# The shared layer's first product and the router's of rounded parts, in a transformer kernel written for one core

## The chip, the core and the metric

The kernel runs on one core of a Trainium2 chip. The core has five engines that work side by side and wait for one another through semaphores: TensorE (PE in the profile; PEld is its weight load), VectorE (DVE), ScalarE (ACT), GpSimd (POOL) and SyncE (SP), whose queue here only issues DMAs. The metric is the time on the device of one execution, in microseconds.

## What is computed

A two-layer model over 16 tiles of 384 tokens, each token 256 numbers. Cut to what matters:

```python
h = edges_of_image_and_text_rows                      # 16 x 384 x 256
h = h + attention(layernorm(h))                       # 16 heads, local window of 128
h = h + top_k_block(layernorm(h))                     # rows of highest score through one product and gelu
h = h + state_space(layernorm(h))                     # a circulant recurrence over 256 states
xf = layernorm(h)
logits = xf @ router_w.T + router_b                   # 8 experts, the top two are taken
shared = gelu(xf @ shared_w1.T + b1) @ shared_w2.T + b2   # 256 -> 1024 -> 256
h = h + shared + sum_e(weight_e * ffn_e(xf))          # experts 256 -> 1024 -> 256
```

## The kernel before

Work goes tile by tile (NB = 16), T = 384 tokens in NT = 3 parts of P = 128. A tile is in one of three stages, and one pass of `sequence(b, ...)` on each engine interleaves them: the attention of tile b, the chain of tile b - 1 (block, state space, router, first shared product, "up"), the second shared product ("down") and the dispatch to experts of tile b - 2; also the head of tile b + 1 (edges, text, norm, queries, keys, values). `sequence` counts slots s = 0 to 32 (SLOTS = 33). In each slot `unit(b, s)` does a step of attention: scores on TensorE (L1624, L1625), their maximum on VectorE (L1150), exponentials on ScalarE (L819), turned probabilities (L1633) and products with the values (L1652). Everything else has its slot by constants such as TURN1 = 12, STATE = 14, CONV = 15, TURN2 = 27, UP = 28, LOGIT = 30. Each engine works through its own list strictly in order; nothing is reordered at run time. Tiles 2 to 13 run in a loop, 0, 1, 14 and 15 are written out; pass NB has the chain alone, with idle products (`keep_warm`, L1834) between the chain's steps. The passes with a chain and a head are those of b = 1 to 14.

What the change touches, in the order of a pass's end: in slot 27 TensorE turns the chain's normalised rows into the accumulator (L1689), ScalarE copies them to `xcT` (L839), VectorE's `keys(b + 1)` writes the rounded keys `k_hi` (L1118) and their rests `k_lo` (L1122), `query_rests` writes `q_lo` (L1129). SyncE's `stack` copies them head by head into `qs` and `ks` (L445, L451), in four groups (`PAIRS`), each with a semaphore `stacked[g]`; the attention units 2g and 2g + 1 are the first to read group g. In slot 28 TensorE does `logits(b - 1)` (L1773), in slot 30 `values(b + 1)` (L1600), whose third part writes to the keys' bank and waits for `k_lo`; then the turn of the context rows `cx` (L1667, after VectorE's L1163), `up(b - 1, 0)`, the output product (L1640), and `up(b - 1, f)` for f = 1 to 7 (L1703), after which the next pass begins. Each `up` writes one of two banks; ScalarE's `hidden_layer` (L855) reads it, and `up` f + 2 waits for that.

Products of fp32 operands show two records each. Operands of type F32R (rounded to fewer bits) show one. The experts' products already use rounded parts: with x = x_hi + x_lo, a product is w_hi x_hi + w_hi x_lo + w_lo x_hi (L1885 to L1889). `rot` and `cum` hold the state space's rotations and sums and, as `trial`, the unread outputs of the rank comparisons (L1221, L1224) with the constant tables `before` and `after`. In pass 0 VectorE also makes the eigenvalues and, in slots 2 to 10, their powers.

## Time and profile before

| | |
|---|---|
| median of three runs | 2078.8 us (2075.1 to 2082.78) |
| the profiled execution | 2077.58 us, span 2075.8 us |
| TensorE busy | 1955.6 us, 94% of the span |
| TensorE's weight loads | 1572.7 us, 76% |
| VectorE, ScalarE, GpSimd busy | 1337.9, 1071.3, 778.8 us |
| first shared product (L1703) | 512 records, 174.5 us busy |
| experts' stage | from about 1465 us to the end |

The columns of the rows below: in the order of time a row has the start (us from the span's start), the duration (of all instructions it merges, from the first start to the last end), the engine (SPq and ACTq are DMA issues), the line of the kernel, the operation, output<-inputs, shapes, the count, and in brackets how long the engine was idle before and what released it. Matmul records overlap; the distance of their starts is what they cost. A busy engine is not one at its peak, and idle time of an engine that sets no end costs nothing.

### The profile page before, as it was taken

The page shows a single profiled execution, that of the slowest core. Times are in us where ns is not written, and L with a number is a line of the kernel's source. Part 1 is how long each engine was busy: PE and PEld are TensorE (multiplying, and loading weights), DVE is VectorE, ACT ScalarE, POOL GpSimd, SP SyncE. Part 2 cuts the span into 40 slices and gives each one's busy share as a digit, 9 for nine tenths or more (in the row PEclk, how much of TensorE's full clock was granted, in tenths as well). Part 3 has the DMA queues.
Part 4 walks back from the last instruction along what each step waited for, and adds up shares of the span by engine and source line. Part 5 has one row for each costly group of instructions (what it writes and reads, how often), then busy time and mean ns, then how long its engine had stood idle before and what let it go on. Part 6 is the DMA issues. An engine that isn't in the chain of part 4 may idle for free.

```text
span 2075.8 us, 45068 instructions
## 1 busy us (share of the span) xinstructions
PE 1955.6 (94%) x13784; PEld 1572.7 (76%) x13864; DVE 1337.9 (64%) x3781; ACT 1071.3 (52%) x2509; POOL 778.8 (38%) x1269
## 2 busy tenths in 40 slices
PE   4779999999999999999999999888999999999997
PEld 3556667667676676666676766666999999999997
DVE  4667677676776776766767767655665555656553
ACT  0445556455455564555645545541554555555553
POOL 4013324333343233332432333304354455555544
PEclk8899999999999999999999999998999999999998
DMA  4221120211212202212022021110442232323222
GB/s 153 62 62 40 39 69 23 61 52 24 69 37 47 68 24 54 56 28 69 30 54 64 28 54 38 32 55 23 128 129 45 45 89 45 89 43 86 48 45 40
DMA packets 81091, 116.56 MB, mean 56 GB/s; under 512 B 20964, under 2 KB 61508, under 8 KB 78724
## 3 DMA queue, kind: packets, MB, share of 16 engines
q1 hardware_dynamic: 54372, 84.16, 14.6%
q0 software_dynamic: 23360, 27.91, 8.0%
q10 hardware_dynamic: 3312, 3.94, 0.7%
q8 instruction: 21, 0.34, 0.1%
q14 instruction: 26, 0.21, 0.0%
HBM read 51.58 MB, written 26.71 MB: 38 GB/s over the span
## 4 chain that ended last, share of the span: by engine, by line
PE 75%; issue 9%; DVE 8%; POOL 4%; ACT 1%; ACTq 1%; POOLq 0%; DVEq 0%; DMA 0%
PE ps L1888 14%; PE ps L1703 8%; PE ps L1716 7%; PE ps L1899 4%; PE ps L1900 4%; PE ps L1901 4%; PE ps L1633 4%; PE ps L1549 3%; PE ps L1625 3%; PE ps L1652 3%; PE ps L1577 2%; PE ps L1694 2%; PE ps L1754 2%; PE ps L1689 2%; PE ps L1624 2%
## 5 line engine op out<-in xcount | busy, mean ns | idle before, releaser
L819 ACT ACTIVATE prob<-ps,mx 128x256 f32<-128x256 f32 (+1 forms) x768 | 294.3, 440 | 188.7 <-DVE mx L1150 176.8
L1150 DVE TENSOR_REDUCE mx<-ps 128x2 f32<-128x512 f32 (+1 forms) x384 | 228.5, 596 | 206.7 <-PE ps L1625 196.8
L931 ACT ACTIVATE hid_hi<-ps,b 128x256 fp32r<-128x256 f32 x408 | 205.9, 505 | 276.3 <-PE ps L1888 276.3
L811 ACT ACTIVATE pT<-ps 128x512 f32<-128x512 f32 (+1 forms) x384 | 202.4, 532 | 136.2 <-PE ps L1633 123.5
L1479 DVE TENSOR_TENSOR hid_lo<-hid_full,hid_hi 128x256 fp32r<-128x256 f32 x408 | 170.9, 425 | 143.3 <-ACT hid_full L934 139.8
L732 POOL DMA_INDIRECT result<-yb,idx_o x102 | 176.8, 1734 | 164.1 <-DVE yb L1496 142.2
L1899 PE MATMUL ps<-w_hi,hid_hi 128*128 128x256 f32 x816 | 230.0, 282 | 0.0
L1900 PE MATMUL ps<-w_lo,hid_hi 128*128 128x256 f32 x816 | 225.5, 276 | 0.0
L1901 PE MATMUL ps<-w_hi,hid_lo 128*128 128x256 f32 x816 | 225.3, 276 | 0.0
L1633 PE MATMUL ps<-ident,prob 128*128 128x128 f32 x1280 | 207.3, 276 | 7.0 <-ACT prob L819 6.8
L934 ACT ACTIVATE hid_full<-ps,b 128x256 f32<-128x256 f32 x408 | 206.2, 505 | 0.0
L1625 PE MATMUL ps<-ks,qs 96*128 96x512 f32 (+1 forms) x384 | 199.0, 518 | 3.1 <-ACT prob L819 3.1
L676 POOL DMA_INDIRECT slot_rows<-pay,row_i x96 | 113.3, 1180 | 219.6 <-DVE tok L1339 195.1
L1633 PEld LDWEIGHTS ps<-ident,prob 128*128 128x128 f32 x1280 | 160.1, 143 | 44.6 <-ACT prob L819 13.7
L1716 PE MATMUL ps<-sw,hid 128*128 128x256 f32 x768 | 185.9, 387 | 2.3 <-ACT g L846 1.0
L1703 PE MATMUL ps<-xcT,sw 128*128 128x384 f32 x512 | 174.5, 495 | 0.0
L1888 PE MATMUL ps<-xg_hi,w_hi 128*128 128x256 f32 x816 | 165.1, 284 | 2.5 <-DVE xg_lo L1472 1.4
L1716 PEld LDWEIGHTS ps<-sw,hid 128*128 128x128 f32 x768 | 138.8, 190 | 34.2 <-issue 11.7
L1888 PE MATMUL ps<-xg_hi,w_lo 128*128 128x256 f32 x816 | 164.4, 283 | 0.0
L1888 PE MATMUL ps<-xg_lo,w_hi 128*128 128x256 f32 x816 | 164.4, 283 | 0.0
L1900 PEld LDWEIGHTS ps<-w_lo,hid_hi 128*128 128x128 f32 x816 | 153.4, 188 | 0.0
L1899 PEld LDWEIGHTS ps<-w_hi,hid_hi 128*128 128x128 f32 x816 | 153.3, 188 | 0.0
(283 smaller groups left out, 4114.5 us busy)
## 6 DMA issues: line engine op xcount, KB each, us to landing
w_raw<-in_w SPq DMA_DIRECT2D x16, 1024.0 KB
xin<-in_x SPq DMA_DIRECT2D x32, 384.0 KB
ks<-k_hi SPq DMA_DIRECT2D x256, 48.0 KB, 2.1
qs<-q_hi SPq DMA_DIRECT2D x120, 96.0 KB, 2.1
ks<-k_lo SPq DMA_DIRECT2D x128, 48.0 KB, 2.1
xn_rows<-xc SPq DMA_DIRECT2D x16, 384.0 KB, 2.5
result<-h SPq DMA_DIRECT2D x16, 384.0 KB
qs<-q_lo SPq DMA_DIRECT2D x60, 96.0 KB, 2.1
```

Source lines behind the costliest of these rows:

```text
L819: ins = act.activation(prob[:, s % PB, hh, w], ps[:, s % 2, hh * 2 * P + w.start:(hh + 1) * 2 * P], ACT.Exp, bias=mx[:, s % 2, hh:hh + 1])
L931: act.activation(hid_hi[:, f], ps[:, f % 4, 0:CHUNK], ACT.Gelu_apprx_tanh, bias=b1[half][:, f:f + 1])
L934: act.activation(hid_full[:, f % 4], ps[:, f % 4, 0:CHUNK], ACT.Gelu_apprx_tanh, bias=b1[half][:, f:f + 1]).then_inc(ehid_ready.sem, 1)
L1150: dve.tensor_reduce(mx[:, s % 2], sc, AX_X, ALU.max, negate=True).then_inc(max_done.sem, 1)
L1625: pe.matmul(dst, qs[:, r, m, i * P:(i + 1) * P], ks[:, r, :, m, keys], start=False, stop=True).then_inc(scores_done.sem, 1)
L1633: ins = pe.transpose(ps[:, 2 + u % 2, (2 * hh + k) * P:(2 * hh + k + 1) * P], prob[:, u % PB, hh, k * P:(k + 1) * P], ident[:])
L1703: ins = pe.matmul(ps[:, 6 + f % 2, 0:T], sw1[:, k, f * P:(f + 1) * P], xcT[:, k], start=(k == 0), stop=(k == KB - 1))
L1716: ins = pe.matmul(tile_out(i), hid[:, f, i * P:(i + 1) * P], sw2[:, f], start=(f == 0), stop=(f == FB - 1))
L1888: ins = pe.matmul(ps[:, f % 4, 0:CHUNK], w[half][:, k, cols], x[:, k], start=(n == 0), stop=(n == len(terms) - 1))
L1899: pe.matmul(out, hid_hi[:, f, rows], w2_hi[half][:, f], start=(f == 0), stop=False)
L1900: pe.matmul(out, hid_hi[:, f, rows], w2_lo[half][:, f], start=False, stop=False)
L1901: ins = pe.matmul(out, hid_lo[:, f, rows], w2_hi[half][:, f], start=False, stop=(f == FB - 1))
```

## The change

The router's and the first shared product take rounded parts. `sw1` is loaded into room of `hid` in pass 0, rounded on ScalarE in slot 12 and its rest taken on VectorE in slot 15; the router's weights are split before pass 1 into `rw_parts`, high and low parts side by side, so one product with `xcT_hi` gives both; a second one with `xcT_lo` adds to the high half, and VectorE adds the two halves and the bias. ScalarE's last copy of turned rows writes `xcT_hi`; VectorE's new `turned_rests` writes `xcT_lo`, between `k_hi` and `k_lo` (or by itself where there are no keys). On TensorE the first two parts of `values` go ahead of the logits, which move from slot 28 to 29. To make room, `k_hi` and `k_lo` share their memory with `rot`, `xcT_hi` with `xcT`, `xcT_lo` with `st`; the rank comparisons write to `st`, `xn` and `cum`; VectorE waits for all four `stacked` groups before it writes `rot` (slot 1 of pass 0, slot 14 of later ones); `before` and `after` become windows into one table each, `rank_cols` lies in `hb2`. The loads of the experts' biases move behind SyncE's pass NB.

```diff
 # memory
-        rank_cols = sb("rank_cols", [P, T])
-        before = sb("before", [P, NT, T], BF16)
-        after = sb("after", [P, NT, T], BF16)
+        before_w = sb("before_w", [P, T + 2 * P], BF16)
+        after_w = sb("after_w", [P, T + 2 * P], BF16)
+        before, after = ([w[:, (NT - 1 - i) * P:(NT - 1 - i) * P + T] for i in range(NT)] for w in (before_w, after_w))
+        rw_parts = sb("rw_parts", [P, KB, 2 * NE], F32R)
+        rw_hi, rw_lo = rw_parts[:, :, 0:NE], rw_parts[:, :, NE:2 * NE]
-        sw1 = sb("sw1", [P, KB, F])
+        sw1_hi = sb("sw1_hi", [P, KB, F], F32R)
+        sw1_lo = sb("sw1_lo", [P, KB, F], F32R)
-        k_hi = room("k_hi", [P, KB, T], F32R)
-        k_lo = room("k_lo", [P, KB, T], F32R)
+        with ExitStack() as shared:
+            xcT_hi = shared.enter_context(nc.sbuf_tensor("xcT_hi", [P, KB, T], F32R))
         xcT = room("xcT", [P, KB, T])
...
+        with ExitStack() as shared:
+            k_hi = shared.enter_context(nc.sbuf_tensor("k_hi", [P, KB, T], F32R))
+            k_lo = shared.enter_context(nc.sbuf_tensor("k_lo", [P, KB, T], F32R))
         rot = room("rot", [P, 4, T])
         cum = room("cum", [P, 2, T])
+        with ExitStack() as shared:
+            xcT_lo = shared.enter_context(nc.sbuf_tensor("xcT_lo", [P, KB, T], F32R))
         st = room("st", [P, 2, T])
...
+        rank_cols = hb2[:].rearrange("p i d -> p (i d)")[:, 0:T]
...
+        sw1 = place[:, 0:KB * F].rearrange("p (k n) -> p k n", k=KB)
 # SyncE: (sw1, t["sw1"]) leaves late_loads
             load_image(1)
+            sp.wait_ge(mats_read.sem, mats_read.at(0, 1))
+            sp.dma_start(sw1, t["sw1"]).then_inc(sw1_loaded.sem, 16)
             load_halo(1)
...
+            sequence(NB, True, True, False, False)
+            sp.wait_ge(hb2_ready.sem, hb2_ready.at(NB, 0))
             for half in range(2):
                 load_biases(half, half)
-            sequence(NB, True, True, False, False)
 # ScalarE
-                act.activation(xcT[:], ps[:, 6:8, 0:T], ACT.Copy).then_inc(xcT_ready.sem, 1)
+                act.activation((xcT if n < 2 else xcT_hi)[:], ps[:, 6:8, 0:T], ACT.Copy).then_inc(xcT_ready.sem, 1)
...
+            def round_shared():
+                act.wait_ge(sw1_loaded.sem, sw1_loaded.at(0, 16))
+                act.activation(sw1_hi[:], sw1, ACT.Copy).then_inc(sw1_rounded.sem, 1)
...
+                    if first and s == TURN1:
+                        round_shared()
 # VectorE
-                for i in range(NT):
-                    dve.tensor_scalar(before[:, i], rank_cols[:], rank_own[:, i:i + 1], None, ALU.is_lt)
-                    dve.tensor_scalar(after[:, i], rank_cols[:], rank_own[:, i:i + 1], None, ALU.is_ge)
+                dve.memset(before_w[:, 0:2 * P], 1.0)
+                dve.memset(after_w[:, 0:2 * P], 0.0)
+                dve.tensor_scalar(before_w[:, 2 * P:], rank_cols, rank_own[:, 0:1], None, ALU.is_lt)
+                dve.tensor_scalar(after_w[:, 2 * P:], rank_cols, rank_own[:, 0:1], None, ALU.is_ge)
...
+            def split_shared():
+                dve.wait_ge(sw1_rounded.sem, sw1_rounded.at(0, 1))
+                dve.tensor_tensor(sw1_lo[:], sw1, sw1_hi[:], ALU.subtract)
+            def split_router():
+                link(dve.tensor_copy(rw_hi, rw[:]), setup_step, 0)
+                dve.tensor_tensor(rw_lo, rw[:], rw_hi, ALU.subtract).then_inc(shared_split.sem, 1)
+            def turned_rests(b):
+                dve.wait_ge(xcT_ready.sem, xcT_ready.at(b, 3))
+                dve.tensor_tensor(xcT_lo[:], ps[:, 6:8, 0:T], xcT_hi[:], ALU.subtract).then_inc(rest_ready.sem, 1)
...
                 ins.then_inc(k_ready.sem, 1)
+                if chained:
+                    turned_rests(b - 2)
                 dve.wait_ge(k_ready.sem, k_ready.at(b, 1))
...
-            trial = [rot[:, 0], rot[:, 1], rot[:, 2], rot[:, 3], cum[:, 0], cum[:, 1]]
+            spare_rows = xn[:].rearrange("p i d -> p (i d)")
+            trials = [[st[:, 0], st[:, 1], spare_rows[:, 0:T], spare_rows[:, T:2 * T], cum[:, 0], cum[:, 1]],
+                      [st[:, 0], st[:, 1], rot[:, 0], rot[:, 1], cum[:, 0], cum[:, 1]]]
...
-                    for i in range(NT):
-                        ins = dve.tensor_tensor(logit[:, i], ps[:, 7, i * NE:(i + 1) * NE], rb_row[:], ALU.add)
-                    ins.then_inc(logit_read.sem, 1)
+                    parts = ps[:, 7, 0:2 * NT * NE].rearrange("p (i n e) -> p i n e", i=NT, n=2)
+                    link(dve.tensor_tensor(logit[:], parts[:, :, 1], rb_row[:].unsqueeze(1).to_broadcast([P, NT, NE]),
+                                           ALU.add), chain_step, b)
+                    dve.tensor_tensor(logit[:], logit[:], parts[:, :, 0], ALU.add).then_inc(logit_read.sem, 1)
...
                     if first and s == 1:
                         eigenvalues()
+                        for pair in range(PAIRS):
+                            dve.wait_ge(stacked[pair].sem, stacked[pair].at(b, stacked[pair].per))
...
+                    if chained and att and s == STATE:
+                        for pair in range(PAIRS):
+                            dve.wait_ge(stacked[pair].sem, stacked[pair].at(b, stacked[pair].per))
...
+                    if first and s == CONV:
+                        split_shared()
...
+                    if chained and not head and s == UP - 1:
+                        turned_rests(b - 1)
...
             dve.wait_ge(late_loaded.sem, late_loaded.at(0, NLATE))
+            split_router()
             sequence(1, True, False, True, True, True)
 # TensorE
-                for k in range(KB):
-                    ins = pe.matmul(ps[:, 6 + f % 2, 0:T], sw1[:, k, f * P:(f + 1) * P], xcT[:, k],
-                                    start=(k == 0), stop=(k == KB - 1))
+                terms = [(w, x, k) for w, x in ((sw1_hi, xcT_hi), (sw1_hi, xcT_lo), (sw1_lo, xcT_hi)) for k in range(KB)]
+                for n, (w, x, k) in enumerate(terms):
+                    ins = pe.matmul(ps[:, 6 + f % 2, 0:T], w[:, k, f * P:(f + 1) * P], x[:, k],
+                                    start=(n == 0), stop=(n == len(terms) - 1))
...
-                    pe.wait_ge(xcT_ready.sem, xcT_ready.at(b, 3))
+                    pe.wait_ge(rest_ready.sem, rest_ready.at(b, 1))
                     for i in range(NT):
+                        first, rows = 2 * NE * i, slice(i * P, (i + 1) * P)
                         for k in range(KB):
-                            ins = pe.matmul(ps[:, 7, i * NE:(i + 1) * NE], xcT[:, k, i * P:(i + 1) * P], rw[:, k],
-                                            start=(k == 0), stop=(k == KB - 1))
+                            pe.matmul(ps[:, 7, first:first + 2 * NE], xcT_hi[:, k, rows], rw_parts[:, k],
+                                      start=(k == 0), stop=False)
+                        for k in range(KB):
+                            ins = pe.matmul(ps[:, 7, first:first + NE], xcT_lo[:, k, rows], rw_hi[:, k],
+                                            start=False, stop=(k == KB - 1))
...
                     if head and s == UP + 2:
-                        values(b + 1)
+                        values(b + 1, 2, NT)
...
+                    if head and s == TURN2 + 1:
+                        values(b + 1, 0, 2)
-                    if chained and s == TURN2 + 1:
+                    if chained and s == TURN2 + 2:
                         logits(b - 1)
...
             pe.wait_ge(late_loaded.sem, late_loaded.at(0, NLATE))
+            pe.wait_ge(shared_split.sem, shared_split.at(0, 1))
             sequence(1, True, False, True, True, first=True)
```

## Rows read from the trace of the kernel before

**Rows 1.** Busy us by stretch: length, PE, PEld, DVE, ACT, POOL; then clock
```profile
96.00:100.00 4.00, 4.00 (x24) 3.10 (x23) 1.38 (x2) 3.13 (x9) 0.00 (x0) 1.00 0.00 1
...
637.00:720.00 83.00, 81.05 (x527) 57.96 (x530) 59.03 (x175) 45.35 (x102) 28.81 (x61) 1.00 0.18 47
```

**Rows 2.** Order of time, end of a steady tile: start, duration, engine, instruction
```profile
620.79 1.40 PE L1773 MATMUL ps<-rw,xcT 128*128 128x8 f32 x12
...
621.84 1.14 DVE L1122 SCALAR_TENSOR_TENSOR k_lo<-ps,bk,k_hi 128x384 fp32r<-128x384 f32 x2
...
622.05 2.84 PE L1600 MATMUL ps<-wv,xT 128*128 128x256 f32 x12
622.89 0.95 DVE L1129 TENSOR_TENSOR q_lo<-xn,q_hi 128x768 fp32r<-128x768 f32 x1
...
624.50 0.42 DVE L1163 TENSOR_TENSOR cx<-cx,sumv 128x256 f32<-128x256 f32 x1
...
624.98 0.44 PE L1667 MATMUL ps<-ident,cx 128*128 128x128 f32 x2
...
627.41 9.19 PE L1703 MATMUL ps<-xcT,sw 128*128 128x384 f32 x28
...
628.90 0.58 ACT L855 ACTIVATE hid<-ps,sb 128x384 f32<-128x384 f32 x1 [1.17 <-PE ps L1703]
...
632.28 1.06 DVE L1063 TENSOR_SCALAR xc<-h,lnc 128x256 f32<-128x256 f32 x3
...
636.44 0.27 PE L1624 MATMUL ps<-mask_bf,ident_bf 128*128 128x256 bf16 x1
```

**Rows 3.** Order of time, fp32r products of 256 and of 512 columns
```profile
1500.76 0.40 PE L1888 MATMUL ps<-xg_lo,w_hi 128*128 128x256 f32 x2
1501.00 0.40 PE L1888 MATMUL ps<-xg_hi,w_lo 128*128 128x256 f32 x2
...
673.69 0.40 PE L1549 MATMUL ps<-gray_lo,band_hi 128*128 128x512 f32 x1
673.92 0.40 PE L1549 MATMUL ps<-gray_hi,band_lo 128*128 128x512 f32 x1
```

**Rows 4.** Order of time, SyncE's last stacking copies of a steady tile
```profile
641.08 1.23 SPq L451 DMA_DIRECT2D ks<-k_lo  x2
```

**Rows 5.** DMA issues of the page: copies, KB each, us from issue to landing
```profile
ks<-k_lo SPq DMA_DIRECT2D x128, 48.0 KB, 2.1
...
sw<-in_sw SPq DMA_DIRECT2D x2, 1024.0 KB, 7.8
```

**Rows 6.** Order of time, tile NB
```profile
1404.34 2.28 DVE L1348 TENSOR_TENSOR w_lo<-w_raw,w_hi 128x2048 fp32r<-128x2048 f32 x1
...
1437.16 10.43 PE L1703 MATMUL ps<-xcT,sw 128*128 128x384 f32 x28
```

**Rows 7.** Order of time, tile 0 and the start of tile 1
```profile
67.57 0.42 DVE L1150 TENSOR_REDUCE mx<-ps 128x2 f32<-128x256 f32 x1
...
74.09 1.22 SPq L451 DMA_DIRECT2D ks<-k_lo  x2
...
75.69 0.42 DVE L1150 TENSOR_REDUCE mx<-ps 128x2 f32<-128x256 f32 x1
...
76.88 0.39 PE L1624 MATMUL ps<-mask_bf,ident_bf 128*128 128x256 bf16 x1 [0.91 <-DMA ks<-k_lo]
...
77.61 0.42 DVE L1150 TENSOR_REDUCE mx<-ps 128x2 f32<-128x256 f32 x1
...
137.62 0.37 PE L1624 MATMUL ps<-mask_bf,ident_bf 128*128 128x256 bf16 x1 [4.77 <-issue]
```

**Rows 8.** Groups of instructions by line: count, then busy us, mean ns of one
```profile
L1900 PEld LDWEIGHTS ps<-w_lo,hid_hi 128*128 128x128 f32 x816 | 153.4, 188 | 0.0
...
L866 ACT ACTIVATE w_hi<-w_raw 128x2048 fp32r<-128x2048 f32 x1 | 1.9, 1896 | 0.0
```

**Rows 9.** Order of time, the setup on ScalarE
```profile
49.70 0.81 ACT L789 ACTIVATE xT<-ps 128x768 f32<-128x768 f32 x1 [18.33 <-remote]
```

More of the change, by code:

```diff
@@ L63 @@
 ROOT_STEPS = 1 + 3 * NEWTON
-CHAIN_STEPS = 17 + ROOT_STEPS
+CHAIN_STEPS = 18 + ROOT_STEPS
 SLOT_STEPS = 6
@@ L424, in build @@
             (wb, t["wb"]), (d_row, t["d"].partition_broadcast(P)), (rw, t["rwT"]),
-            (rb_row, t["rb"].partition_broadcast(P)), (sw1, t["sw1"]), (sw2, t["sw2"]), (sb1, t["sb1"]),
+            (rb_row, t["rb"].partition_broadcast(P)), (sw2, t["sw2"]), (sb1, t["sb1"]),
             (sb2_row, t["sb2"].partition_broadcast(P)),
@@ L913, in _ @@
             act.wait_ge(u_gathered.sem, u_gathered.at(0, 16 * (NB - 1)))
-            sequence(0, True, False, False, True)
+            sequence(0, True, False, False, True, first=True)
             act.wait_ge(late_loaded.sem, late_loaded.at(0, NLATE))
@@ L1209, in chain @@
             def chain(b, s, last):
+                trial = trials[last]
                 if s == RANK:
@@ L1384, in sequence @@
                     if head and s == UP - 1:
-                        keys(b + 1)
+                        keys(b + 1, chained)
+                    if chained and not head and s == UP - 1:
+                        turned_rests(b - 1)
                     if head and s == UP:
@@ L1426, in _ @@
             normalise_rows(0)
-            keys(0)
+            keys(0, False)
             query_rests(0)
@@ L1590, in keys, with values @@
                 project(b, wk, 2)
-            def values(b):
+            def values(b, first, last):
                 pe.wait_ge(ctx_ready.sem, ctx_ready.at(b, 0))
-                for i in range(NT):
+                for i in range(first, last):
                     if i == 2:
@@ L1600, in values @@
                         ins = pe.matmul(dst, xT[:, k, i * P:(i + 1) * P], wv[:, k], start=(k == 0), stop=(k == KB - 1))
-                ins.then_inc(proj_done.sem, 1)
+                if last == NT:
+                    ins.then_inc(proj_done.sem, 1)
             def values_sum(b, first, last):
@@ L1850, in _ @@
             keys(0)
-            values(0)
+            values(0, 0, NT)
             matrices()
```

12 lines of the change are left out of this document (8 added, 4 removed).

## The prediction

> **What bounds the kernel now.** I read the busy time by stretches first, then the order of time inside one image tile, then the waits. In a steady tile TensorE is busy for 81.05 of 83 us at the full clock [rows 1]. No other engine comes near that, so a step taken off TensorE's own row of work counts in full, and a step put on another engine counts only where TensorE has to wait for it. The end of a tile is the place to read [rows 2]. VectorE makes the rounded keys (up to 621.8), their rests (621.84), the rests of the queries (622.89) and the context rows (624.50 to 624.92). TensorE meanwhile does logits (620.79), values (622.05), and at 624.98 turns the context rows. The twelve value records (0.24 us apart) end just when VectorE hands over: neither has slack. Then come the eight products of the shared layer, f = 0 right behind the turn and f = 1 to 7 from 627.41 without a gap to 636.44, where the next tile starts. The next tile needs VectorE's normalised rows, ready at 633.3, so there VectorE is about 3 us early.
>
> **The shared product.** Each f is two fp32 products, four records, now. 28 records fill 627.41 to 636.44 [rows 2], 0.3225 us each, 1.29 us per f. Afterwards each f is six fp32r products of 384 columns, one record each, since fp32r products in this kernel show one record where fp32 shows two. Their pitch at 384 columns isn't in the trace. The experts' fp32r products of 256 columns start 0.24 us apart for two, 0.120 us each [rows 3]; at 2.4 GHz 256 columns are 0.107, so 13 ns are lost on each. The edge products of 512 columns are 0.23 to 0.24 apart against 0.213: some 20 ns lost. The fp32 record, two passes of 384 columns, loses only 2.5 ns (0.3225 against 0.320). So the pitch lies between 0.1625 and 0.182. I take 0.170, between the experts' loop, which has the same form, and the fp32 record, which has the same width: 1.02 us per f, 0.27 saved on each, 2.16 us a tile. ScalarE keeps up: it needs 0.58 us per f and starts (628.90) 0.2 after TensorE has gone on to the next f (628.70) [rows 2], so one f could be as short as about 0.85 us before ScalarE set the pace.
>
> The Trainium skill, "TensorE: Matmul & The Clock Gate", section "Back-to-back issue gap", gives an isolated warm gap of N/2.4 plus 2.5 ns; by it the pitch would be 0.1625. The fp32 record agrees with it to the nanosecond, the experts' rows [rows 3] are 11 ns slower; the case it would make is the second rival.
>
> **The rests of the turned rows.** `turned_rests` is one VectorE subtraction of 768 elements, and sits between the rounded keys and their rests. The same form is 0.95 us long, and the operation behind it starts 0.87 later, or 0.95 at most (the one at 622.89) [rows 2]. It reads two buffers where the new one reads the accumulator, as the operation at 621.84 does at the same rate per element. I take 0.87. It delays key rests, query rests and context rows on VectorE. The key rests are awaited by TensorE's third value tile, and that is why two value tiles go ahead of the logits: eight records from 620.7 to 622.7, then the logits (12 records before and after; their small column count makes them bound by weight loads, 0.10 each, so I count no change), then four value records to 624.95. So TensorE arrives at the context turn when it did before, and VectorE 0.87 later: a new idle of 0.85 to 0.87 us. The SyncE queue wants the query rests only after the first group's rounded keys, near 627, and they would be there at 624.7, and VectorE's normalised rows slip to 634.4 while TensorE comes at 635.1: both covered, the latter by only 0.7 us. The logits' two dependent additions in place of three independent ones cost VectorE about 0.1 in that cover. Net per steady tile: 2.16 - 0.87 = 1.3 us. Fourteen tiles have this pattern: **-18.2 us**. If the pitch is 0.1625 the tile gains 1.65, at 0.182 it gains 0.7.
>
> **The stacking copies can't take it back.** SyncE issues a tile's last key copy by 642.3 [rows 4], it lands 2.1 us after issue [rows 5], at 644.4. The unit that needs it starts ten microseconds later. VectorE's new waits for the stacks at slot 14 (about 667) find them done: nothing. What they guard is that keys and rotations now share room.
>
> **Last two tiles.** In tile NB - 1 and in the last one there are no keys; the rests stand bare between ScalarE's copy and the logits, 1.0 us, and the eight f save 2 to 2.5 (some run at half clock: 28 records took 10.43 us in the last tile [rows 6] where steady ones take 9.03). -1.5 and -1.4: **-2.9 us**.
>
> **The first tile pays.** There, VectorE gets four waits at slot 1, for all stacked keys and queries of tile 0, ahead of its maximum for unit 1. Today it does that maximum at 67.57 [rows 7]. The last key copies of that tile are issued at 74.09 and after, and TensorE sees them at 76.88, having idled 0.91 for them. Queued behind VectorE's waits are the powers of the eigenvalues and every maximum, and for each maximum ScalarE's exponentials and TensorE wait. It isn't made good: from slot 2 to 10 VectorE is itself the pace (maxima at 75.69 and 77.61, 1.92 apart, with the powers between them and no gap). So 76.8 - 67.6 = 9.2, less some 0.3 of waiting that it now has at slot 2: **+8.9 us**, full, since nothing later in tile 0 stands at a fixed time. Bounds: 5 (if the first slots run closer together than that pace) and 9.3.
>
> Also in tile 0: the weights' rounding on ScalarE, 2048 columns, 1.9 us [rows 8], and their subtraction on VectorE, 2.28 us [rows 6], both between units of attention. Bounds 0 and 4.2; TensorE is busy for 4.00 of the 4 us from 96 to 100, VectorE for 1.38, ScalarE for 3.13 [rows 1], so most of VectorE's part is covered and about half of ScalarE's isn't; I take +1.5. Before tile 1 TensorE now waits for `split_router`, behind VectorE's last copy of tile 0 (its end is near 138.0) and two operations on 16 and 8 columns, some 0.5 us with the wait between them. Today its first unit starts at 137.62 [rows 7]: **+0.9 us**. Together the first tile: **+11.3 us** (6 to 15).
>
> **At nothing.** Four fewer operations for `before` and `after` (about 1 us on VectorE near 29 us) are hidden: whatever comes before, ScalarE starts `xT` at 49.70 after 18.33 us of a remote wait [rows 9]. The 1 MB load of `sw1` moves behind `mats_read` (a read of tile 0's start, long past), on SyncE behind the stacking copies and tile 1's image: issued near 77, and with the 7.8 us to landing of its like [rows 5] there by 85, before the rounding at slot 12, which is past 90 today and later then. The halo load behind it waits for grays made 15 us later. Bias loads move behind `hb2_ready`, far ahead of the experts. The rank trials have the same sizes in other places. The experts' stage, the last 610 us, isn't touched.
>
> **Sum.** -18.2 - 2.9 + 11.3 = -9.8 us. The profiled execution took 2077.6 us (span 2075.8), so 2067.8 there. It was 1.2 us under the median of 2078.8 of the three runs, which gives 2069.0.
>
> **Rivals.**
> 1. The first tile's stall is absorbed (VectorE catches up in slots 2 to 10, or the stacks land sooner): -18.7, 2060. For: TensorE itself waited for stacks three times there. Against: VectorE's row from 70 to 88 us has no gaps.
> 2. The rounded products lose only 2.5 ns, like the fp32 record: 14 x 1.65 + 3.6 - 11.3 = -15.4, 2063.4. For: the same width. Against: every fp32r row loses more.
> 3. Slower: fp32r products with a new stationary tile each time are paced by the weight load, 0.188 us long in its records [rows 8], 6 x 0.19 = 1.14 us per f. The tile gains 1.2 - 0.87 = 0.33, in all 5.7, and the first tile's 11.3 decides: +5.6, 2084.4. It decides from a pitch of 0.182 up, where 16 tiles save just what the first tile costs: that is the upper bound above. Against: the experts' products run at 0.120 with the same loads [rows 3], so the loads overlap.
> 4. VectorE's normalised rows become what the next tile waits for: their cover of 0.7 us goes if the inserted work is longer than 1.6 us. It would cap the tile's gain near 1: 2073. That the rounding does not do what it says (VectorE's 0.87 cancels TensorE's gain) is the same case with a gain of 0.7 at most: 2079.
>
> **Chances.** Forecast (2065 to 2073) 0.50; rival 1 0.10; rival 2 0.15; rival 4 0.12; rival 3 0.08; the rest, above all a first tile that costs still more, 0.05. The range of 8 in 10 reaches from rival 1 to somewhat below rival 3: 2058 to 2081. A measurement of this kernel can tell about 0.5% from no change, here 10.4 us, so the border is at 2068.4, inside the forecast's own range. Faster: not quite half of the forecast, and rivals 1 and 2: 0.46. Slower by over 10.4 us needs rival 3 and a dear first tile: 0.08. Same: 0.46.
>
> **What the profile after would show.** The up products: 42 records for f = 1 to 7 in about 7.1 us, and a pitch to be read directly. TensorE idle of 0.85 us before it turns `cx`, released by VectorE; none before the turn of the normalised rows. A tile period of 81.3 us in place of 82.6. In tile 0, VectorE's second maximum at about 77 in place of 67.57. The start of tile 1 about 11 us later. What would make this wrong: an fp32r pitch outside 0.16 to 0.18, a stall in tile 0 that is made good, or ScalarE's remote wait at 31 to 50 us coming out shorter or longer.

## The result

The changed kernel took 2084.15 us (median of 17 runs, 2080.66 to 2087.36), the kernel before 2080.03 us (17 runs, 2072.70 to 2082.78): a ratio of 1.0022, with a 95% interval of 1.0013 to 1.0031. The forecast was 2069.0, with a range of 2058 to 2081; the time is 15 us above the one and 3 us outside the other. By the border of 0.5% the change makes no difference; the small loss of 4 us can be told from zero.

The profiled execution of the changed kernel took 2085.0 us (span 2083.2, against 2075.8 before). These lines of its page answer to the rows of before:

```profile
PE 1951.3 (94%) x14040; PEld 1629.1 (78%) x14120; DVE 1355.8 (65%) x3782; ACT 1072.1 (51%) x2510; POOL 780.4 (37%) x1269
...
L1964 PE MATMUL ps<-w_hi,hid_hi 128*128 128x256 f32 x816 | 233.5, 286 | 0.0
L1966 PE MATMUL ps<-w_hi,hid_lo 128*128 128x256 f32 x816 | 229.4, 281 | 0.0
L1965 PE MATMUL ps<-w_lo,hid_hi 128*128 128x256 f32 x816 | 229.3, 281 | 0.0
```

The last three are the experts' second product, which the change does not touch. In the kernel before the same three groups were

```profile
L1899 PE MATMUL ps<-w_hi,hid_hi 128*128 128x256 f32 x816 | 230.0, 282 | 0.0
L1900 PE MATMUL ps<-w_lo,hid_hi 128*128 128x256 f32 x816 | 225.5, 276 | 0.0
L1901 PE MATMUL ps<-w_hi,hid_lo 128*128 128x256 f32 x816 | 225.3, 276 | 0.0
```

That is four to five nanoseconds more on each of 2448 products. These durations overlap; the pitch, the time from one start to the next, is what counts. From the first to the second line of each of the next pairs (start, duration) it is thirty products, in the kernel before and then in the changed one:

```profile
1518.72 0.28 PE L1899 MATMUL ps<-w_hi,hid_hi 128*128 128x256 f32 x1
...
1522.12 0.28 PE L1899 MATMUL ps<-w_hi,hid_hi 128*128 128x256 f32 x1
```

```profile
1517.26 0.28 PE L1964 MATMUL ps<-w_hi,hid_hi 128*128 128x256 f32 x1
...
1520.79 0.28 PE L1964 MATMUL ps<-w_hi,hid_hi 128*128 128x256 f32 x1
```

They take 3.40 us and 3.53 us. The stage works in 51 chunks of token rows, each with 48 products of this kind. Over a whole chunk (its last start less its second, over the products between) the pitch is 0.1135 before and 0.1177 after, in every one of the 51 chunks. The first product keeps its 0.120 us. A chunk from turn to turn takes 11.65 us before and 11.85 after (length, then busy us of each engine, granted clock):

```profile
1506.28:1517.93 11.65, 11.65 (x102) 11.65 (x101) 5.95 (x15) 5.95 (x18) 6.59 (x8) 1.00 0.63 198
```

```profile
1504.62:1516.47 11.85, 11.85 (x103) 11.85 (x101) 6.07 (x15) 5.95 (x18) 7.05 (x8) 1.00 0.66 200
```

The granted clock is full in both (1.00, the third number from the end), and the other engines do nearly the same work. The two traces side by side, cut at landmarks: VectorE's operation that fills `vaug` for tile n ("the mark of tile n"; the pass of tile n - 1 ends there), and the first expert product, from which to the end of the span I count the experts' stage.

| stretch | before | after | difference |
|---|---|---|---|
| span start to the mark of tile 0 | 61.11 | 61.48 | +0.4 |
| tile 0 | 69.55 | 77.08 | +7.5 |
| tile 1 | 77.44 | 80.42 | +3.0 |
| tiles 2 to 14, 13 periods | 1085.51 | 1076.48 | -9.0 |
| mark of tile 15 to the first expert product | 171.75 | 167.71 | -4.0 |
| experts' stage | 610.4 | 620.0 | +9.6 |
| span | 2075.8 | 2083.2 | +7.4 |

So all that comes ahead of the experts gained 2.2 us where the sum said 9.8, and a stage that the sum put at nothing lost 9.6.

The end of a steady tile, in order of time, answers to [rows 2] (start, duration, engine, instruction, idle time before it and what ended it). The lines from 634.52 on show what follows, taken from the tile before:

```profile
709.82 1.14 DVE L1158 TENSOR_SCALAR k_hi<-ps,bk 128x384 fp32r<-128x384 f32 x2 [1.05 <-PE ps L1633]
710.88 0.95 DVE L1151 TENSOR_TENSOR xcT_lo<-ps,xcT_hi 128x768 fp32r<-128x768 f32 x1
711.74 1.13 DVE L1164 SCALAR_TENSOR_TENSOR k_lo<-ps,bk,k_hi 128x384 fp32r<-128x384 f32 x2
712.79 0.95 DVE L1171 TENSOR_TENSOR q_lo<-xn,q_hi 128x768 fp32r<-128x768 f32 x1
...
714.40 0.43 DVE L1205 TENSOR_TENSOR cx<-cx,sumv 128x256 f32<-128x256 f32 x1
...
714.88 0.44 PE L1724 MATMUL ps<-ident,cx 128*128 128x128 f32 x2 [0.53 <-DVE cx L1205]
...
634.52 0.70 PE L1761 MATMUL ps<-xcT_hi,sw_hi 128*128 128x384 f32 x2
635.06 0.52 PE L1761 MATMUL ps<-xcT_lo,sw_hi 128*128 128x384 f32 x2
635.41 0.51 PE L1761 MATMUL ps<-xcT_hi,sw_lo 128*128 128x384 f32 x2
...
642.08 0.28 PE L1681 MATMUL ps<-mask_bf,ident_bf 128*128 128x256 bf16 x1
```

The 42 records for f = 1 to 7 fill 634.52 to 642.08, 7.56 us where the 28 of before filled 9.03; two of them take 0.35 us from start to start (635.06 to 635.41). The subtraction stands between the rounded keys and their rests, and TensorE idles 0.53 us, for VectorE, before it turns `cx`. The rests of the keys (711.74) start 1.92 us after the rounded keys (709.82). In the kernel before it was 1.18, 0.74 less: the rests stood at 621.84 [rows 2], the rounded keys here:

```profile
620.66 1.14 DVE L1118 TENSOR_SCALAR k_hi<-ps,bk 128x384 fp32r<-128x384 f32 x2 [1.04 <-PE ps L1577]
```

Tile 0, answering to [rows 7]:

```profile
76.25 0.42 DVE L1192 TENSOR_REDUCE mx<-ps 128x2 f32<-128x256 f32 x1 [8.22 <-DMA ks<-k_lo]
76.71 0.63 ACT L836 ACTIVATE prob<-ps,mx 128x128 f32<-128x128 f32 x2 [8.28 <-DVE mx L1192]
...
77.39 0.39 PE L1681 MATMUL ps<-mask_bf,ident_bf 128*128 128x256 bf16 x1 [7.40 <-ACT prob L836]
...
78.45 0.41 DVE L1192 TENSOR_REDUCE mx<-ps 128x2 f32<-128x256 f32 x1
```

VectorE's second maximum is at 76.25 where it was at 67.57; ScalarE and TensorE stand behind it in turn.

### The profile page after: what moved, and what is told of

Same layout as the page of the kernel before. It is cut to its first block, busy times and chain, and to the rows that moved or that the text cites. A ratio compares the mean times of both kernels' runs of the same rounds, so it can differ in the third digit from the quotient of the medians.

```text
span 2083.2 us, 45657 instructions
## 1 busy us (share of the span) xinstructions
PE 1951.3 (94%) x14040; PEld 1629.1 (78%) x14120; DVE 1355.8 (65%) x3782; ACT 1072.1 (51%) x2510; POOL 780.4 (37%) x1269
## 4 chain that ended last, share of the span: by engine, by line
PE 66%; issue 11%; DVE 10%; POOL 9%; ACT 1%; DMA 1%; POOLq 1%; ACTq 1%; DVEq 0%
PE ps L1953 14%; PE ps L1761 7%; PE ps L1965 5%; PE ps L1966 5%; PE ps L1964 5%; POOL slot_rows L693 3%; PE ps L1605 3%; PE ps L1690 3%; PE ps L1682 2%; PE ps L1774 2%; PE ps L1709 2%; PE ps L1633 2%; PE ps L1751 2%; PE ps L1812 2%; PE ps L1746 2%
## 5 line engine op out<-in xcount | busy, mean ns | idle before, releaser
L1966 PEld LDWEIGHTS ps<-w_hi,hid_lo 128*128 128x128 f32 x816 | 153.2, 188 | 0.0
```

Source lines behind the costliest of these rows:

```text
L1966: ins = pe.matmul(out, hid_lo[:, f, rows], w2_hi[half][:, f], start=False, stop=(f == FB - 1))
```

## The experiments

The theories after this reading. For the experts' stage, A: the place of its buffers does it. The change takes 1536 + 2048 bytes per partition out of the persistent tensors and puts 8192 + 128 in, so that every buffer of that stage lies 4736 bytes further up. Its rivals: the place of TensorE's instructions, since the changed stream is longer, or a state that one chunk hands on to the next. For the tiles: the stall at slot 1 costs tile 0 its 7.5 us, the wait for the router's parts costs tile 1, and the subtraction's place takes back part of the gain in each steady tile.

### Buffers of the experts' stage moved

```
+            b1 = [room(f"b1_{j}", [P, FB]) for j in range(2)]
+            b2_row = [room(f"b2_row{j}", [P, D]) for j in range(2)]
+            room("gap", [P, 656])
             ones1 = room("ones1", [P, NE])
...
-            b1 = [room(f"b1_{j}", [P, FB]) for j in range(2)]
-            b2_row = [room(f"b2_row{j}", [P, D]) for j in range(2)]
+            room("hole", [P, 528])
```

The experts' biases go first, so that their early loads meet nothing still in use; the gap makes up the rest of the 4736 bytes, and `hole` keeps the room that the biases had.

> The kernel before, with the experts' buffers (parts of the weights, of the hidden rows, of the gathered rows) 4736 bytes per partition further up, which is where the changed kernel has them; the experts' biases stand ahead of them. Nothing else differs. The experts' stage of the changed kernel is 620.0 us against 610.4 us, though none of its instructions is changed: the second product's starts stand 0.1177 us apart and not 0.1133 us (48 a chunk, 51 chunks, 10.8 us). Theory A, the place of the buffers does it: about 9.6 us slower than the kernel before (2089.6), second product 0.1177 us apart, the tiles' stage as it was. Rival B, the place does nothing and the difference is the instruction stream's or the tiles' stage's doing: 2080.0 within 2 us and 0.1133 us apart.

Measured: 2087.42 us (6 runs), ratio to before 1.0040 (1.0022 to 1.0058). The span is 2082.5, the experts' stage 620.2, all 51 chunks at a pitch of 0.1177: theory A. Its page has the changed kernel's numbers in the old kernel:

```profile
L1901 PE MATMUL ps<-w_hi,hid_hi 128*128 128x256 f32 x816 | 233.5, 286 | 0.0
L1903 PE MATMUL ps<-w_hi,hid_lo 128*128 128x256 f32 x816 | 229.4, 281 | 0.0
L1902 PE MATMUL ps<-w_lo,hid_hi 128*128 128x256 f32 x816 | 229.3, 281 | 0.0
```

The move of the buffers alone brings the whole loss of the stage into the kernel before.

> The changed kernel with the experts' buffers 3456 bytes further up than it has them, 8192 bytes above their place in the kernel before, so that every one has the same address modulo 8192 as before. Theory A (the place, by its lower address bits): the second product back at 0.1133 us, 2084.2 - 9.6 = 2074.6 us, so 5 us faster than the kernel before once only the buffers' place is taken out. Rival A2, the distance from the bottom of the memory matters and not the lower bits: 0.1177 us or worse, 2084. Rival B (not the place): 2084.2 and 0.1177 us.

Measured: 2078.36 us (10 runs), 5.8 less than the changed kernel; ratio to before 0.9994 (0.9981 to 1.0008). The stage took 615.8 us, and neither theory had said that: the pitch was 0.1177 in the first chunk, 0.1138 in the second, and so in turn through all 51. Part of the loss came back with the address modulo 8192, less than theory A had said (2074.6). The loop's buffers and instructions are the same in every chunk but for which of two sets of weights it reads, and that changes with the expert, not with the chunk; so the place of the buffers can't be all.

> The kernel before with the experts' buffers 8192 bytes further up (the biases ahead of them, as in the run with 4736 bytes). With 4736 bytes all 51 chunks had the second product's starts 0.1177 us apart (0.1135 before), and the changed kernel with its buffers at the addresses of before modulo 8192 had 0.1177 in every other chunk and 0.1138 in the ones between, so an address modulo 8192 isn't all. Theory A3 (lower address bits together with the place of the instruction stream): the stream is that of before, so 0.1135 in all chunks, span 2075.8 within 3. Rival A4 (any move of these buffers can turn it): 0.1177 in all or half of the chunks, span 2080 to 2085.

Measured: 2077.85 us (one run), span 2076.1, stage 615.9, the same alternation. That is A4's pattern, at a span that A3 allowed; TensorE's stream was untouched.

> As the run with 8192 bytes, with 128 bytes more; 4736 and 8320 are both 128 modulo 512. Theory A3 with the address modulo 512 as what decides: 0.1177 us in all chunks, experts' stage 620 us. Rival, larger strides decide (4736 is 640 modulo 4096, 8320 is 128 modulo 4096): 0.1135 us, 610 us.

Measured: 2086.58 us (one run), span 2084.8, stage 620.1, 0.1177 in all chunks, as the theory said; 128 bytes more make the difference to the run before. Which stride decides isn't shown: besides 0 and 8192 only moves that are 128 modulo 512 were tried.

> The kernel before with only the hidden rows' buffers (and the results' buffer behind them) 4736 bytes further up; the weights and the gathered rows stay. The first product, which writes none of them, keeps its 0.120 us in every kernel so far; only the product that reads the hidden rows changes. Theory: the hidden rows' place decides, 0.1177 us in all chunks and 620 us for the stage. Rival: the weights' place, or the two against each other, decides: 0.1135 us and 610 us if the weights' own, either if it is their distance.

The edit is a gap of 4736 bytes ahead of `hid_full` alone. Measured: 2086.02 us (one run), span 2084.2, stage 619.6, 0.1177 in all chunks. Moving the hidden rows alone (with the results' buffer `yb` behind them) is enough. They are the stationary operand of the second product.

### TensorE's instructions moved, and time shifted

```
             pe.wait_ge(proj_loaded.sem, proj_loaded.at(0, NPROJ))
+            for _ in range(5):
+                pe.wait_ge(proj_loaded.sem, 1)
             queries(0)
```

The traces count three TensorE instructions more with these five waits (16217 for 16214), and 16 and 64 more with the 31 and 127 waits of the runs below.

> The kernel before with five waits, long fulfilled, ahead of the first tile's projections in TensorE's stream, so that all that follows lies some instructions further on; no buffer moves. Theory A (buffers alone): 0.1135 us in all chunks, 610 us for the experts' stage. Rival C (where the loop's instructions lie): the second product at 0.1177 us in all chunks or in every other one, 615 to 620 us.

Measured: 2082.45 us (one run), span 2080.7, stage 615.9, the alternation again, without a buffer moved.

> The kernel before with 16 waiting instructions, long fulfilled, ahead of the projections in TensorE's stream, no buffer moved. With three, every other chunk was slow. Theory C1 (the place modulo some power of two of at most 16 instructions): all chunks at 0.1135 us, stage 610 us. Theory C2 (a larger distance, or none): some or all at 0.1177, 615 or 620 us.

Measured: 2079.84 us (one run), span 2078.1, stage 616.1, alternating.

> The same with 64 instructions. Theory C1, and C2 with a distance of 32 or 64 instructions: all chunks at 0.1135 us, 610 us. Otherwise some or all at 0.1177 us, 615 or 620 us.

Measured: 2077.08 us (one run), span 2075.3, stage 610.5, 0.1135 in all chunks.

> The changed kernel with three waiting instructions, long fulfilled, ahead of the projections in TensorE's stream, no buffer moved. If the stream's place is what made its experts' stage 9.6 us longer, such a move can undo it: 0.1135 in all or every other chunk, stage 610 or 615 us, span 2073.6 or 2078.4. If its buffers' place holds it there whatever the stream: 0.1177 in all, 620 us, span 2083.

Measured: 2084.66 us (one run), span 2082.9, stage 619.6: three chunks at 0.1135, then 0.1177 to the end. The stream's place didn't free the changed kernel.

> The kernel before with one memset of 384 elements on VectorE ahead of its first chunk of the experts' stage, so that VectorE comes some 0.2 us later to the first turned rows, once; TensorE's stream and all buffers are where they were. Moving TensorE's stream alone, or the buffers alone by 8192 bytes, made the second product's starts 0.1177 us apart in every other chunk. Theory D (a state that a chunk hands on to the next, tipped by any shift of time): again 0.1177 in some or all chunks, stage 615 to 620 us. Rival (only the place of TensorE's instructions or operands can tip it): 0.1135 in all chunks, stage 610.4 us, span 2075.8 within 4.

Measured: 2075.60 us (one run), span 2073.8, stage 610.7, 0.1135 in all chunks. This shift of time tipped nothing.

> The changed kernel once more, not altered, for a second profile. If the pattern of the second product's starts belongs to the kernel: 0.1177 us in all 51 chunks, experts' stage 620.0 us. If it is thrown anew in each execution: some chunks at 0.1135, 610 to 618 us.

Measured: 2083.96 us, span 2082.2, stage 620.1, 0.1177 in all chunks, as in its first profile.

> The changed kernel with the three edits once more, not altered, for a second profile. If the pattern belongs to the kernel: 0.1177 us in every other chunk, beginning with the first, stage 616.0 us. If it is thrown anew in each execution: another pattern, 610 or 620 us.

Measured: 2063.47 us, span 2061.7, stage 610.6. The first profile of the same kernel (below) had the alternation and 615.9. The page of the first, and then that of the second:

```profile
L1965 PE MATMUL ps<-w_hi,hid_hi 128*128 128x256 f32 x816 | 231.9, 284 | 0.0
L1966 PE MATMUL ps<-w_lo,hid_hi 128*128 128x256 f32 x816 | 227.5, 279 | 0.0
```

```profile
L1965 PE MATMUL ps<-w_hi,hid_hi 128*128 128x256 f32 x816 | 230.0, 282 | 0.0
L1966 PE MATMUL ps<-w_lo,hid_hi 128*128 128x256 f32 x816 | 225.5, 276 | 0.0
```

So one kernel can show both patterns, and the runs with longer streams show nothing by themselves: each was one execution, and 0.1135 or the alternation could have come up in either. The two profiles come from two chips, so the chip is a rival to the single execution. Against it: on the chip of the first profile four executions of this kernel took 2062.75, 2063.01, 2068.13 and 2071.25 us, the last with the alternation, the first two near the 2063.47 that had 0.1135 on the other chip. Counting all 20 profiles sorts it:

| buffers of the experts' stage | profiles | stage, us | pattern |
|---|---|---|---|
| as before, or 8192 bytes above | 10 | 610.4 to 610.8 in five, 615.8 to 616.1 in five | all chunks 0.1135, or every other 0.1177 and 0.1138 between |
| 4736 or 8320 bytes above, or only the hidden rows 4736 | 10 | 619.4 to 620.2 | 0.1177 in all, in three profiles but for the first three chunks |

No profile of either row shows the other's pattern. In profiles, then, the buffers' place decides between the rows; within the first, something that I can't name decides. That other executions at the slow addresses never do better isn't shown: two of the kernels below have single times far under their medians, 2068.47 for 2074.49, and 2076.49 and 2076.90 for 2081.85, about what the alternation would save, and none of these was profiled. The patterns may also account for part of the wide spread of the kernel before (2072.70 to 2082.78): its own profile, 2.5 us under the median, caught the best one. That its slower runs had the alternation isn't shown either.

### The first tile

```
-                        for pair in range(PAIRS):
-                            dve.wait_ge(stacked[pair].sem, stacked[pair].at(b, stacked[pair].per))
...
-                dve.tensor_scalar(rot[:, 0, 0:m], turn[:, 0, 0:m], re, None, ALU.mult)
+                dve.tensor_scalar(cum[:, 0, 0:m], turn[:, 0, 0:m], re, None, ALU.mult)
```

(and the same for the other uses of `rot` in `powers`)

> The changed kernel, but the powers of the first tile keep their partial products in cum, which no stacking transfer reads, so that VectorE's two waits for the stacked keys and queries in the second slot of tile 0 are gone. The first theory: the wait costs what tile 1's first context rows are late by, 7.5 to 7.9 us, all of it comes back and the time is 2076.5. Rival: the stall covers for waits that stand in the same tile anyway (the rounding of the shared weights, ScalarE's rows, the router's parts), and only part comes back, 2 to 5 us: 2079 to 2082. The experts' stage stays at 620.0 us by both.

Measured: 2074.49 us (10 runs), 9.7 less than the changed kernel, ratio to before 0.9969 (0.9958 to 0.9981). By the marks tile 0 took 68.82 us and not 77.08: the stall costs 8.3 (the seven profiles with it have 76.7 to 78.0 there, the four without it 68.8 to 69.9). Of the remaining 1.4 us, 0.6 lie in the experts' stage (619.4), whose first three chunks had the short pitch; two executions differ by the rest anyway. Those four still contain the rounding of the shared weights, and the kernel before with its variants has 68.0 to 69.6 in nine profiles. The means are 69.5 and 68.7, so the rounding costs at most some 0.8 us, and no run has it alone.

```
                 if n == 2 and head:
                     pe.wait_ge(xT_ready.sem, xT_ready.at(b + 2, 1))
+                if n == 2 and isinstance(b, int) and b == 0:
+                    pe.wait_ge(shared_split.sem, shared_split.at(0, 1))
...
-            pe.wait_ge(shared_split.sem, shared_split.at(0, 1))
```

> The changed kernel, but TensorE waits for the router's parts before the last turn of the first tile's chain and not ahead of tile 1's first scores. TensorE's idle time ahead of tile 1's first scores was 4.77 us before and 6.84 us after. First theory: those 2.1 us come back and with them part of the 3.0 us that pass 1 lost while the granted clock was 0.74 for 40 us (0.93 and 1.00 before): 2 to 5 us, 2079 to 2082. Rival: VectorE itself, late with its rows, sets that time, and nothing comes back: 2084.

Measured: 2081.85 us (10 runs), 2.3 less; ratio to before 1.0007 (0.9995 to 1.0020). TensorE's wait ahead of tile 1, in the changed kernel and then with this edit (us in total, times, longest):

```profile
PE ps L1681 <- DVE rw_parts L1146: 6.8, 1, 6.8
```

```profile
PE ps L1681 <- issue: 4.8, 1, 4.8
```

The idle is 2.1 us shorter: the first theory. The rest of what tile 1 gains goes with the clock. The same 20 us a little into tile 1 (length; PE, PEld, VectorE, ScalarE, GpSimd; granted clock), first in the changed kernel, then with the edit:

```profile
157.60:177.60 20.00, 17.86 (x119) 11.59 (x122) 14.14 (x37) 15.19 (x44) 6.67 (x18) 0.74 0.02 5
```

```profile
157.60:177.60 20.00, 16.59 (x125) 10.69 (x122) 14.44 (x38) 13.91 (x38) 6.67 (x18) 0.93 0.05 12
```

After the longer idle the granted clock spends more of this stretch at the lower of its two levels, 1.2 GHz. Tile 1 took 80.42 us with the wait in front and 77.57 without, the 77.44 of before.

### The steady tile

```
                 dve.wait_ge(xcT_ready.sem, xcT_ready.at(b, 3))
+                dve.tensor_tensor(cum[:], ps[:, 6:8, 0:T], xcT_hi[:], ALU.subtract)
                 dve.tensor_tensor(xcT_lo[:], ps[:, 6:8, 0:T], xcT_hi[:], ALU.subtract).then_inc(rest_ready.sem, 1)
```

> The changed kernel with VectorE's subtraction of the turned rows done twice (the first time into cum, which nothing reads then). The prediction priced that instruction at 0.87 us a tile on the path (VectorE is late ahead of the last context rows, and TensorE idles 0.53 us before it turns them). By that each tile of the steady stretch takes 0.87 to 0.95 us more, 83.25 for 82.37, and the kernel 12 to 14 us more, span 2096. Rival: that stretch has 0.5 us of cover elsewhere, so 0.4 us a tile, 6 us in all.

Measured: 2100.93 us (one run), span 2099.2, 16 more. The shortest periods are 83.12 to 83.18 where the changed kernel has 82.37: 0.78 us for the instruction. The mean is 84.1 against 82.6 (periods between the marks of tiles 3 and 14): two of three tiles are 1.3 to 1.7 us longer than the shortest. Waits of TensorE in two tiles of it:

```profile
PE ps L1833 <- DVE xcT_lo L1152: 1.8, 2, 0.9
PE ps L1747 <- DVE xc L1088: 1.2, 2, 0.6
PE ps L1725 <- DVE cx L1206: 1.1, 2, 0.5
```

The wait ahead of `cx` is no longer than in the changed kernel. The second subtraction is paid at a new place: TensorE waits 0.9 us for `xcT_lo` ahead of the logits, where the changed kernel waits 0.03. So this run prices a subtraction that both the logits and `cx` stand behind; that the one of the changed kernel costs its time at `cx` is tested by the next run.

The changed kernel itself has two such long tiles among the eleven, in both of its profiles; in the first they take 83.97 and 83.93 us, and one begins at 550.2. The first line lies at its very start:

```profile
549.00:552.00 3.00, 3.00 (x10) 2.73 (x10) 2.71 (x18) 2.25 (x3) 0.00 (x0) 0.50 0.46 96
550.00:560.00 10.00, 10.00 (x52) 9.55 (x52) 6.72 (x29) 4.86 (x9) 2.30 (x3) 0.89 0.41 86
560.00:570.00 10.00, 9.64 (x51) 7.22 (x51) 4.55 (x19) 5.46 (x12) 0.00 (x0) 1.00 0.28 61
```

TensorE is busy throughout, and the granted clock is 0.50, its lower level, for some 3 us right behind the idle of 0.53 us ahead of `cx` (which ends at 548.54); 0.89 is the mean over ten. The same profile has two more such falls, at 217.5 to 221.5 (0.57) and 1211.0 to 1214.5 (0.51): one in each of tiles 2, 6, 10 and 14. The nine profiles of the kernel before and its variants, with 0.10 us of idle ahead of `cx`, have no such tile.

```
-                    if head and s == UP:
+                    if head and s == UP + 2:
                         query_rests(b + 1)
```

> The changed kernel, but VectorE makes the rest of the queries (0.95 us) after the last context rows of a tile and not ahead of them. Theory: the rest of the turned rows costs what it does because it stands in front of those context rows; with another 0.95 us out of the way TensorE's 0.53 us idle before it turns them goes, 0.5 us a tile, 7 us in all, span 2076. Rival: the next tile's scores wait for the stacked query rests, which start 2 us later, and the time goes up, by 0.5 to 1.5 us a tile, span 2090 to 2105.

Measured: 2071.52 us (one run), 12.6 under the changed kernel's median; span 2069.7, 13.5 under its profile's, all of it ahead of the experts (stage 620.2). The theory's place was right and its size too small: the period is 81.55 to 81.58 in every steady tile, 0.80 less and not 0.5, and there are no long ones. The larger waits of TensorE in two tiles of the kernel before, of the changed kernel, and with this edit:

```profile
PE ps L1689 <- DVE xc L1063: 1.3, 3, 0.6
PE ps L1633 <- ACT prob L819: 0.9, 2, 0.4
```

```profile
PE ps L1746 <- DVE xc L1088: 1.4, 3, 0.6
PE ps L1724 <- DVE cx L1205: 1.1, 2, 0.5
PE ps L1690 <- ACT prob L836: 0.9, 2, 0.5
```

```profile
PE ps L1746 <- DVE xc L1088: 1.2, 2, 0.6
PE ps L1690 <- ACT prob L836: 0.9, 2, 0.5
```

The wait for `cx` is gone, and the scores of the next tile wait for nothing new.

### Put together

First the edits of `powers`, of the router's wait and of the buffers (8192 bytes above their old place):

> The changed kernel with three of the earlier edits together: the powers' partial products in cum (9.7 us less alone), TensorE's wait for the router's parts ahead of the chain's last turn (2.3 us less alone), the experts' buffers 3456 bytes further up (5.8 us less alone). If they add up: 2084.2 - 17.8 = 2066.4 us. If the second product's state is a matter of luck that any edit throws anew: 2066 with half the chunks at 0.1135, 2062 with all of them, 2071 with none.

Measured: 2065.57 us (4 runs, 2062.75 to 2071.25), ratio to before 0.9934 (0.9908 to 0.9960). They add up. The profiled execution, with the alternation, was the 2071.25. Then with the query rests late as well:

> The changed kernel with the three edits and the rest of the queries made after the last context rows. If the terms add up (12.6 us less for the last one alone): 2065.6 - 12.6 = 2053 us, 1.2 per cent faster than the kernel before. If the first tile's stall and the late rests share cover: 2056 to 2060.

Measured: 2051.62 us (4 runs), ratio to before on the same chip 0.9870 (0.9842 to 0.9898), some 27 us faster than the kernel before and 32 faster than the changed one. Its profile had 0.1135 in all chunks, stage 610.8, and no fall of the clock in its steady tiles.

## Why the prediction was wrong, step by step

**The experts' stage "isn't touched".** This step failed. The profiled execution missed its forecast (2067.8) by 17.2 us, and this step alone is 9.6 of them. No instruction of it was touched; its addresses were, by 4736 bytes, because its room begins where the persistent tensors end. The move alone costs the kernel before 0.40%, 8.3 us. The trace of before could have warned: its second product has a pitch of 0.1135 and its first one of 0.120 [rows 3], for the same shapes, so something other than the shape sets it. It isn't the whole miss, though. With the buffers 8192 bytes above their old place the changed kernel took 2078.36 us, inside the range, and its ratio to the kernel before of 0.9994 (0.9981 to 1.0008) shows no gain, where 9.8 us were forecast. The rest of the miss is the steady tiles.

**The pitch of the up products, 0.170.** It is 0.1757, inside the bounds: 1.054 us per f, 0.236 saved on each and not 0.27, 1.89 us a tile and not 2.16. I had weighed the Trainium skill, "TensorE: Matmul & The Clock Gate", section "Back-to-back issue gap"; its 2.5 ns over N/2.4, given there for an isolated product, stand against 15.7 ns in the chains of this trace, and the trace decides. Rival 2 (0.1625) and rival 3 (the weight load's 0.188 or 0.19) both fall. The time that rival 3 gave, 2084.4, is the measured one by chance; its mechanism, a pitch above 0.182, isn't what happened.

**The subtraction, 0.87.** The place was right: it stands between the rounded keys and their rests, and TensorE idles for VectorE ahead of `cx`. It delays VectorE by 0.74 us there and not by 0.87, because it fills part of a distance that stood between the two steps before. The idle is 0.53 us and not 0.85, since TensorE too comes later, by 0.3 us, 0.10 of them in the logits, which take 1.36 us and not 1.26. The whole price in the sum is 1.89 - 1.11 = 0.78; one more subtraction costs 0.78 too (at another wait), and taking as long a step away from there gave 0.80 back. Net gain of an undisturbed steady tile: 1.11 us (82.37 against 83.48), where the forecast was 1.3. The periods that I gave there, 82.6 and 81.3, were misread; the difference is what the sum rests on.

**Fourteen tiles, -18.2.** Thirteen periods lie between the marks of tiles 2 and 15, and they gave 9.0. Of the 9.2 that are missing, 2.5 are the gain of 1.11 for 1.3 in thirteen tiles; 5.5 belong to the four falls of the clock, which the prediction had put at nothing by leaving them out; 1.3 is the fourteenth tile, which falls into the next stretch. Tiles 6 and 10 lose 1.6 us each by the clock. Tile 14 loses 1.6 too: it took 83.23 (82.76 before), and 81.57 to 81.63 in four profiles where the clock held. Tile 2 gained 0.4 (84.11 against 84.54) where 1.11 was due, 0.7 less; it took 82.87 and 82.88 in two profiles where the clock held. How many falls there are differs between executions: the second profile of the changed kernel has three, and its thirteen periods are 2.5 us shorter. Rival 4 named a gain near 1 us a tile, but by VectorE's normalised rows, and TensorE waits no longer for them than before: its number is close, its mechanism isn't there.

**The last tiles, -2.9.** From the mark of tile 15 to the first expert product 4.0 us less, for these 2.9 and the fourteenth tile's 1.3 together. But the kernel before with only its experts' buffers moved had 168.3 us there where its own profile had 171.7, at a granted clock of 0.93 and not 0.90 and with the same instructions. The term can't be tested to a microsecond.

**The first tile, +11.3.** Nearly right as a sum, 7.5 in tile 0 and 3.0 in tile 1, and wrong in its parts. The stall is 8.3 (forecast 8.9, bounds 5 and 9.3). The rounding, put at +1.5, costs at most some 0.8. That the parts' errors nearly cancel is luck. The wait for `split_router`, put at +0.9, costs 2.9: 2.1 of idle, because VectorE's last rows of tile 0 end after TensorE would have started, and 0.8 that go with the clock. Rival 1, the stall absorbed, falls.

**At nothing, right:** the stacking copies and the moved loads don't show up in TensorE's waits of a steady tile. Over two tiles the wait for `cx` is the only new one; the others are as long as before to 0.1 us.

As a sum: 9.6 in the experts' stage, 9.2 in the steady tiles, less 1.1 in the last tiles and 0.4 ahead of tile 2, 17.3 us of the 17.2.

## What to carry to other kernels

A stage whose instructions are untouched is only untouched if its buffers stay where they are: list the addresses before and after, and look whether a tight loop of products moved. Here the pitch differed between loops of the same shape, and one loop had more than one value from execution to execution: where you see that, take several profiles, and don't put a small ratio down to the change until the untouched stages have been compared. And a new instruction on an engine that hands over just in time is paid at every tile, here 0.78 us for one of 0.95; look for another step on that engine that can go behind the handover. Here that gave more than the change had lost.

## What the runs showed of the hardware

- One loop of fp32r products, 128x128 by 128x256, runs at 0.1135 or at 0.1177 us a product, constant through the 48 of a chunk (0.1138 in the short chunks of the alternation), while the other engines' work is nearly the same; over 51 chunks the pattern is all short, alternating, or (nearly) all long, 610, 616 and 620 us for the stage. As far as 20 profiles go, the place of the hidden rows' buffers decides whether the long one comes; one kernel has shown both of the others, in two executions. The mechanism is open: no profile shows what one chunk hands to the next.
- An fp32r product of 384 columns has a pitch of 0.1757 us in chains of six, one record each; at 256 columns it is 0.120 where the stationary tile comes from the weights and 0.1135 or 0.1177 where it comes from the hidden rows. The fp32 product of 384 columns took 0.645 us, in two records.
- An idle of half a microsecond a tile ahead of `cx`, on an engine busy for 97% of the tile, went along with falls of the granted clock to its lower level (0.50 from 549 to 552 us), right behind that idle, at about 1.6 us of time each, in two of eleven tiles of either profile of the changed kernel. With that idle gone there were none, and with 0.9 us more idle they came in two of three tiles. What makes the clock fall in one tile and not in the next isn't shown.
